# Attention's 0/1 selection matrices stored by ScalarE in the first graph sum and loaded by SyncE; gather indices taken further ahead; the decoder laid over all 128 rows

## The reference, cut to what matters

```python
def gcn_conv(x, src, dst, ew, W, b):
    deg = segment_sum(ew, dst, num_segments=N)
    dis = where(deg > 0, rsqrt(maximum(deg, 1e-12)), 0.0)
    norm = dis[src] * ew * dis[dst]
    return segment_sum(norm[:, None] * (x @ W)[src], dst, num_segments=N) + b
h = relu(gcn_conv(layernorm(x), src, dst, ew, W1, b1))     # 64 features
z = relu(gcn_conv(h, src, dst, ew, W2, b2))                # 32 features
x = x + sigmoid(relu(z @ Wd1 + bd1) @ Wd2 + bd2)           # decoder: 32 -> 64 -> 256
...
ft = (layernorm(x) @ W).reshape(n, 8, 32)                  # attention
e = leaky_relu(a1[src] + a2[dst], 0.2)
ex = exp(e - segment_max(e, dst, n)[dst])
out = segment_sum(ft[src] * (ex / segment_sum(ex, dst, n)[dst])[:, :, None], dst, n)
x = x + elu(out)
```

## Time and profile before

| | us |
|---|---|
| median of 3 runs | 9041.6 |
| lowest and highest run | 9036.97, 9072.32 |
| profiled execution, its own time | 9062.31 |
| its span, first to last instruction | 9060.6 |
| first graph sum, gathers | 562 to 2644 |
| second graph sum, gathers | 2796 to 4884 |
| decoder | 4889 to 5060 |
| mixture and projection | 5060 to 5893 |
| attention | 5893 to 8326 |
| the rest (elu, choice, feed-forward) | 8326 to 9061 |

### The profile page before, as it was taken

The page is one execution under the profiler, slowest core; times in us unless marked ns, Lnnn a source line. Parts: engine busy times, 40 slices in busy tenths (PEclk is TensorE's granted clock), DMA queues, the critical chain, the costliest instruction groups (busy, mean ns, idle before and its releaser), DMA issues. The chain is left out here.

```text
span 9060.6 us, 136786 instructions
## 1 busy us (share of the span) xinstructions
PE 5409.2 (60%) x23137; PEld 4141.3 (46%) x23138; DVE 4883.5 (54%) x14105; ACT 1604.5 (18%) x3526; POOL 5076.7 (56%) x5289
## 2 busy tenths in 40 slices
PE   4744444444453444444436899868888888885079
PEld 3643333333343333333334455645656556554046
DVE  6854444444443333333334433278888888888831
ACT  1200000000000000000002333423333333333511
POOL 0037777777754777777774000067677677774241
PEclk5555555555555555555555799977787787787589
DMA  3111111111102000000000000244444444443420
GB/s 71 33 28 26 26 26 26 26 26 26 26 18 72 13 13 13 13 13 13 13 13 8 16 21 19 71 125 130 128 132 132 127 130 128 131 130 107 142 76 20
DMA packets 380970, 523.06 MB, mean 58 GB/s; under 512 B 148710, under 2 KB 278046, under 8 KB 380700
## 3 DMA queue, kind: packets, MB, share of 16 engines
q0 software_dynamic: 198928, 349.25, 15.0%
q1 hardware_dynamic: 180812, 170.51, 6.0%
q10 hardware_dynamic: 960, 0.00, 0.0%
HBM read 450.68 MB, written 68.72 MB: 57 GB/s over the span
## 5 line engine op out<-in xcount | busy, mean ns | idle before, releaser
L694 POOL DMA_INDIRECT conv_rows<-table,conv_idx x3328 | 3157.1, 949 | 1181.5 <-issue 1010.9
L747 PE MATMUL conv_pm<-conv_rows,conv_sel 128*128 x7040 | 1704.5, 415 | 2539.9 <-SPq L710 2539.9
L747 PEld LDWEIGHTS conv_pm<-conv_rows,conv_sel 128*128 128x128 f32 x7040 | 1566.9, 328 | 2677.5 <-issue 2677.5
L1572 POOL DMA_INDIRECT att_rows<-ft_rows,att_idx x1760 | 1693.8, 962 | 1704.4 <-ACT att_idx L1586 1168.3
L736 DVE TENSOR_TENSOR acc<-acc,conv_pm 128x64 f32 (+1 forms) x3520 | 718.2, 204 | 2012.6 <-PE conv_pm L747 1223.2
L1748 PE MATMUL att_pm<-att_rows,att_sel 128*128 128x264 f32 x3520 | 1272.7, 503 | 229.1 <-DVE sums L1884 178.3
L720 DVE TENSOR_SCALAR conv_sel<-iota,edges,edge_w 128x128 f32<-128x128 f32 x3528 | 1014.3, 357 | 493.1 <-issue 467.1
L1748 PEld LDWEIGHTS att_pm<-att_rows,att_sel 128*128 128x128 f32 x3520 | 772.7, 244 | 582.9 <-DVE sums L1884 359.2
L1884 DVE TENSOR_TENSOR sums<-sums,att_pm 128x264 f32 x1760 | 748.3, 425 | 165.8 <-PE att_pm L1748 111.5
L682 ACT ACTIVATE conv_idx<-sources 128x8 int32 x416 | 86.7, 208 | 4000.1 <-SPq L710 3018.7
L1853 DVE TENSOR_TENSOR att_rows<-att_rows,att_pwi 128x1056 f32<-128x1056 f32 x440 | 545.9, 1241 | 10.8 <-issue 10.3
(11 more groups left out here) (357 smaller groups left out, 5993.6 us busy)
## 6 DMA issues: line engine op xcount, KB each, us to landing
att_bc<-places SPq DMA_DIRECT2D x110, 512.0 KB
conv_rows<-table,conv_idx POOLq DMA_INDIRECT x3328, 2.3
att_rows<-ft_rows,att_idx POOLq DMA_INDIRECT x1760
ft_rows<-proj_ft SPq DMA_DIRECT2D x25, 544.0 KB, 3.0
x_normal<-elu_xr SPq DMA_DIRECT2D x25, 514.0 KB
x_spilled<-x_rows SPq DMA_DIRECT2D x25, 512.0 KB, 2.9
elu_xg<-x_spilled SPq DMA_DIRECT2D x25, 512.0 KB
t_xg<-x SPq DMA_DIRECT2D x24, 512.0 KB
```

What stands on the lines that cost most here:

```text
L694: pool.indirect_dma_start(out=rows[:, k, :], out_offset=None, in_=table, in_offset=bass.IndirectOffsetOnAxis(ap=idx[:, k:k + 1], axis=0)). ...
L747: ins = nc.tensor.matmul(pm[q][:, i, :], sel[:, q * QUAD + i, :], rows[:, ds(slots[i], 1), :].rearrange("p a c -> p (a c)"), start=True, s ...
L1572: pool.indirect_dma_start(out=rows[:, k, :], out_offset=None, in_=K.ftd, in_offset=bass.IndirectOffsetOnAxis(ap=idx[:, k:k + 1], axis=0)). ...
```

## The change

**First graph sum.** With `keep=True` (conv1 alone) ScalarE also makes the unweighted selection matrices of all 1760 steps: |destination - column| by eight Abs operations for a section, then Relu(1 - that) over all eight, and stores the section's two quads to DRAM, through two buffers `hot`. In both sums the index ring has four sections instead of sixteen, and a copy waits for gathers up to 24 before its section.

**Attention.** `hots` and its semaphore are gone. SyncE loads each quad's matrices from DRAM; the load of quad q for block b + 1 is issued when TensorE has done quad q of block b. The index ring has 18 sections, filled at the start and refilled one whole ring ahead; GpSimd itself waits for TensorE (`mm_done`) before it gathers into used slots.

**Decoder.** The four windows' 32 latent features lie side by side on the 128 rows: one transpose for the group instead of four, and four matmuls of 128 columns with a zero-padded Wd1 of 128 rows instead of one of 512 columns with 32 rows. `dt` and Wd2 are padded with zeros to 128 rows. The bias is loaded four times and Wd1 four times.

```diff
-def graph_sum(nc, K, name, table, acc, C, x=None):
+def graph_sum(nc, K, name, table, acc, C, x=None, keep=False):
+    AHEAD = 4 * SECT
...
-        idx = ph.sb("idx", [P, SLOTS], I32)
+        idx = ph.sb("idx", [P, AHEAD], I32)
+        hot = ph.sb("hot", [P, 2, SECT, P]) if keep else None
+        stored = [ph.sem(f"stored{h}") for h in range(2)]
...
         @block.scalar
         def _(act):
+            def ones_of(b, j):
+
+                first, half, section = b * AHEAD + j * SECT, j % 2, b * (AHEAD // SECT) + j
+                act.wait_ge(stored[half], (b * (AHEAD // SECT // 2) + j // 2) * 16 + 16)
+                for k in range(SECT):
+                    ins = act.activation(hot[:, half, k, :], K.iota[:, :], ACT.Abs,
+                                         bias=K.edges[:, 1, ds(first + k, 1)], scale=-1.0)
+                ins.then_inc(apart, 1)
+                act.wait_ge(apart, section + 1)
+                act.activation(hot[:, half, :, :], hot[:, half, :, :], ACT.Relu, bias=K.ones[:, 0:1], scale=-1.0
+                               ).then_inc(made, 1)
+                act.wait_ge(made, section + 1)
+                act.dma_start(K.seld[ds(section * 2, 2)].rearrange("q p f -> p q f"),
+                              hot[:, half, :, :].rearrange("p (q i) n -> p q (i n)", i=QUAD)).then_inc(stored[half], 16)
...
+            with act.Fori(0, TB * P // AHEAD) as b:
+                for j in range(AHEAD // SECT):
+                    t = b * AHEAD + j * SECT
                     act.wait_ge(mm_done, t + (UNROLL - LAG + 1))
-                    act.wait_ge(arrived, t + SECT)
+                    act.wait_ge(arrived, t + (SECT + LANES - AHEAD))
                     act.activation(idx[:, j * SECT:(j + 1) * SECT], K.srct[:, ds(t, SECT)], ACT.Copy
                                    ).then_inc(idx_ready, 1)
+                    if keep:
+                        ones_of(b, j)
+            if keep:
+                for b in range(TB * P // AHEAD, STEPS // AHEAD):
+                    for j in range(AHEAD // SECT):
+                        ones_of(b, j)
+                for h in range(2):
+                    act.wait_ge(stored[h], 16 + STEPS // SECT // 2 * 16)
...
-        w1t, b1t = ph.sb("w1t", [CH2, CH1]), ph.sb("b1t", [CH1, 1])
-        w2t, b2t = ph.sb("w2t", [CH1 + 1, D]), ph.sb("b2t", [CH2, 1])
+        w1t, b1t = ph.sb("w1t", [P, GW, CH1]), ph.sb("b1t", [CH1, 1])
+        w2t, b2t = ph.sb("w2t", [P, D]), ph.sb("b2t", [P, 1])
-        zt = [ph.sb(f"zt{i}", [CH2, GW * P]) for i in range(2)]
-        dt = [ph.sb(f"dt{i}", [CH1 + 1, GW * P]) for i in range(2)]
+        zt = [ph.sb(f"zt{i}", [P, P]) for i in range(2)]
+        dt = [ph.sb(f"dt{i}", [P, GW * P]) for i in range(2)]
...
+            for i in range(GW):
+                sp.dma_start(b2t[i * CH2:(i + 1) * CH2, :], b2.unsqueeze(1)).then_inc(loaded, 16)
+            sp.wait_ge(zeroed, 1)
+            for i in range(GW):
+                sp.dma_start(w1t[i * CH2:(i + 1) * CH2, i, :], wd1).then_inc(loaded, 16)
...
             def turn(g, h):
                 pe.wait_ge(scaled, g + 1)
+                nc.tensor.transpose(pt[:, :], u[h][:, :, :].rearrange("p w c -> p (w c)"), K.ident[:, :]).then_inc(turned, 1)
+
+            def widen(g, h):
                 for i in range(GW):
-                    ins = nc.tensor.transpose(pt[:, i * P:(i + 1) * P], u[h][:, i, :], K.ident[:, :])
-                ins.then_inc(turned, 1)
-
-            def widen(g, h):
-                nc.tensor.matmul(pd[:, :], w1t[:, :], zt[h][:, :], start=True, stop=True).then_inc(d_done, 1)
+                    ins = nc.tensor.matmul(pd[:, i * P:(i + 1) * P], w1t[:, i, :], zt[h][:, :], start=True, stop=True)
+                ins.then_inc(d_done, 1)
...
+            def selections(n, q):
+
+                sp.dma_start(sel[:, q * QUAD:(q + 1) * QUAD, :].rearrange("p i n -> p (i n)"),
+                             K.seld[ds(n * NQ + q, 1)].rearrange("a p f -> p (a f)")).then_inc(sel_loaded[q], 16)
...
+            def body(b, more, most, further):
                 if most:
                     sp.wait_ge(m_ready, b + 2)
                     flags(b + 2)
-                    if not isinstance(b, int) or b + 3 < NB:
+                for q in range(NQ):
+                    if q == 2 and further:
                         sp.wait_ge(t_ready, b + 3)
                         places(b + 3)
-            blocks(sp, body)
+                    if more:
+                        sp.wait_ge(mm_done, b * SEGS + (q + 1) * QUAD)
+                        selections(b + 1, q)
...
-            def section(turn, j):
-
-                pool.wait_ge(idx_ready, turn * SECTS + j + 1)
+            def section(n, j, free=None):
+
+                pool.wait_ge(idx_ready, n + 1)
+                if free is not None:
+                    pool.wait_ge(mm_done, free)
...
                     act.wait_ge(mm_done, b * SEGS + (k + 1) * SECT)
-                    if not isinstance(turn, int) or 2 * b + k + SECTS < STEPS // SECT:
-                        take(b * 2 + (k + SECTS), (2 * i + k) % SECTS)
+                    if not isinstance(turn, int) or 2 * b + k + AHEAD < STEPS // SECT:
+                        take(b * 2 + (k + AHEAD), 2 * i + k)
...
-                    pe.wait_ge(sel_ready, b * NQ + q + 1)
+                    pe.wait_ge(sel_loaded[q], b * 16 + 16)
...
-            def hots(n, q):
-
-                s, at = n * SEGS + q * QUAD, q * QUAD
-                tt(sel[:, at:at + QUAD, :], count.unsqueeze(1).to_broadcast([P, QUAD, P]),
-                   K.edges[:, 1, ds(s, QUAD)].unsqueeze(2).to_broadcast([P, QUAD, P]), ALU.is_equal
-                   ).then_inc(sel_ready, 1)
...
+        K.seld = dram("selections", [STEPS // QUAD, P, QUAD * P])
```

More of the change, by code:

```diff
@@ L669, in graph_sum @@
         gathered = [ph.sem(f"gathered{k}") for k in range(LANES)]
-        idx_ready, taken, sel_ready, mm_done, added, arrived, zeroed, x_loaded = (
-            ph.sem(x_) for x_ in ("idx_ready", "taken", "sel_ready", "mm_done", "added", "arrived", "zeroed", "x_loaded"))
+        idx_ready, taken, sel_ready, mm_done, added, arrived, zeroed, x_loaded, apart, made = (
+            ph.sem(x_) for x_ in ("idx_ready", "taken", "sel_ready", "mm_done", "added", "arrived", "zeroed", "x_loaded",
+                                  "apart", "made"))
         block = ph.block()
@@ L875, in scale @@
                                   ).then_inc(scaled, 1)
+            own.did(dve.memset(w1t[:, :, :], 0.0))
+            own.then(dve.memset(w2t[CH1:P, :], 0.0))
+            dve.sem_inc(zeroed, 1)
             for h in range(2):
+                own.then(dve.memset(dt[h][CH1:P, :], 0.0))
                 dve.memset(dt[h][CH1:CH1 + 1, :], 1.0).then_inc(ones_set, 1)
@@ L902, in _ @@
             act.wait_ge(ones_set, 2)
-            act.wait_ge(loaded, 16 * 5)
+            act.wait_ge(loaded, 16 * LOADS)
             def latent(g, h):
@@ L944, in _ @@
             turn(1, 1)
-            pe.wait_ge(loaded, 16 * 5)
+            pe.wait_ge(loaded, 16 * LOADS)
             widen(0, 0)
@@ L1475, in attention @@
     PERIOD, LONG = 3, 9
+    AHEAD = 2 * LONG
     H1 = HD + 1
@@ L1544, in flags @@
                                  ).then_inc(th_loaded, 16)
+            def selections(n, q):
+                sp.dma_start(sel[:, q * QUAD:(q + 1) * QUAD, :].rearrange("p i n -> p (i n)"),
+                             K.seld[ds(n * NQ + q, 1)].rearrange("a p f -> p (a f)")).then_inc(sel_loaded[q], 16)
             places(0)
+            for q in range(NQ):
+                selections(0, q)
             sp.wait_ge(set_up, 1)
@@ L1553, in _ @@
             places(2)
-            def body(turn, i, more, most):
-                b = block_of(turn, i)
+            def body(b, more, most, further):
                 if most:
@@ L1646, in weights @@
                 act.activation(pw, df[:, 0:P], ACT.Exp).then_inc(p_ready, 1)
-            act.activation(count, K.iota[:, :], ACT.Copy).then_inc(counted, 1)
-            for j in range(SECTS):
+            for j in range(AHEAD):
                 take(j, j)
@@ L1922, in body @@
                 where = places(b, 2)
-                if more:
-                    hots(n, 0)
                 add(b, 2, where)
```

68 lines of the change are left out of this document (35 added, 33 removed).

## The result

| | before | after |
|---|---|---|
| median of 4 runs, us | 9047.1 (9037.0 to 9072.3) | 8947.3 (8938.5 to 8952.3) |
| profiled execution / span, us | 9062.3 / 9060.6 | 8945.5 / 8943.8 |
| first gather to last, first sum | 2081.5 | 2080.7 |
| last gather of the first sum to ScalarE's first operation of the next stage | 13.2 | 26.1 |
| gathers, second sum | 2087.3 | 2080.4 |

The ratio of the medians is 0.9882, 95% interval 0.9867 to 0.9898: faster by 1.2%. The spans differ by 116.8 us: 12.9 lost behind the first sum, and 0.8, 6.9, 39.4 and 87.1 gained in both sums' gathers, the decoder and the attention. All the other stages together take 4.5 us more. The central forecast asked for 176 us; 117 came by the two spans and 100 by the medians, since the profiled execution of before was 15 us above its own median.

What follows compares the result with a forecast made beforehand. It took GpSimd's gather issue to bound the graph sums, late feeding and release the attention, and low-clock TensorE the decoder. Terms 15 - 141 - 50 = -176 us gave 8866 us; own range 8817 to 8900, with rivals 8810 to 8960.

Steps and rivals of the forecast that it cites:

- The first sum: First graph sum: ScalarE's new sections of 4.1 us stay hidden until the end, then a tail costs +15 us.
- about twelve of them behind the last gathers: First graph sum, sign of being right: ScalarE's sections take 4 to 5 us, about twelve behind the last gathers.
- The bound of 5.5 us: First graph sum, upper bound: a ScalarE section takes 5.5 us, each dynamic address costing some 0.17, giving +33 us.
- the third rival: First graph sum: ScalarE becomes the bound, from 10.0 us a section; at 12 us, +240, 9282 us; chance 0.05.
- The second sum: Second graph sum: only the index ring gets shorter, so the time changes by 0.
- The decoder: Decoder: using all rows lifts TensorE's granted clock from 0.50 to 1.00, VectorE is the next bound; -50 us.
- the group: Decoder: a group of four windows falls from 6.46 to 4.2 us, 25 groups giving 56 us before 6 are deducted.
- The attention: Attention: without compares and with earlier release, blocks fall from 21.6 us to near GpSimd's issue floor of 20.0; -141 us.
- With some jitter I take 20.35: Attention: block time taken as 20.35 us, from 20.25 plus jitter; 107 x 1.25 = 134 us saved.
- the two-block loop: Attention: gathers, landing, a1, scans, TensorE's sums and next block's first eight steps take 40.5 us, 20.25 a block.
- The handoff: Attention: GpSimd is released by TensorE itself instead of through ScalarE's index copy, 1.0 us earlier.
- the second rival: Attention: bursts of loads delay gather landings, loop 1.2 us longer, 20.95 us a block; -112, 8930 us; chance 0.21.

Runs made afterwards that it cites:

- experiment 5: Two kernels: changed kernel with the decoder's wide product at 65 rows (decoder 157.1 us); kernel before with only that product padded to 128 rows (147.6 us).
- the 65-row run: Changed kernel with the decoder's wide-product operands (dt, w2t) at 65 rows again, all else kept but their zeroing; decoder 157.1 us.
- experiment 6: Changed kernel, but in the first sum ScalarE makes two sections of selections beside each of the first twelve index copies; 11985.7 us beside 11944.2 before.
- the run without reloads: Changed kernel loading only the first block's attention selections, used for all blocks; the run without the standstill took 8951.8 us beside 9049.2 before.
- experiment 1: Changed kernel loading only the first block's attention selections, used for all blocks; first run 12124.8 us beside 12107.6 before, second 8951.8 beside 9049.2.
- the handoff alone, second run: Kernel before with attention indices 18 sections ahead and GpSimd waiting for TensorE itself, compares kept on VectorE; second run 11905.1 us beside 11960.6 before.
- experiment 7: Kernel of experiment 6, with attention's GpSimd waiting for the matmuls of overwritten slots by four gathers instead of eight; 11377.9 us beside 11960.6 before, ratio 0.9516.

## Why the prediction was right or wrong

**The first sum was right.** Section 4.08 us against 4.1, stage end 13 us later against 15. An Abs of 128x128 took 386 ns (363 by the line through the two rows), the Relu 1148 (1120), the issue 0.38 (0.34). Thirteen sections ran behind the last index copy (2607.0), as in the sum; only the last four of them ended behind the last gather's start, so the sign "about twelve of them behind the last gathers" was wrongly worded. The bound of 5.5 us had no ground: no run shows 0.17 us for a dynamic address, and eight Abs take 2.44 us with dynamic addresses (inside the loop) and without (in the tail). Nor had the third rival (ScalarE as the bound): ScalarE waited some 6.2 us ahead of each section.

**The second sum** gained 6.9 us where I had 0. GpSimd waits for nothing there in either kernel; its gathers took 950.4 ns in the mean before and 946.2 after, which is the 6.9 us. In experiment 5's second kernel, whose second sum is the old one, they took 945.2, though under the standstill. So nothing shows that the change did it.

**The decoder was right in cause, 11 us off in size.** The clock rose, and experiment 5 shows that the rows did it. By the Trainium skill, "TensorE: Matmul & The Clock Gate", section "Why this matters for your kernels", being continuously busy would be enough; the 65-row run, busy 136 of 139 us at 0.52, disagrees, as the decoder of before did. The mis-sized term is the group: 4.47 us in the mean and not 4.2. Even at a granted 1.00 it is 4.45 to 4.58, for no engine is full (VectorE is busy 63.6 of 85 us and TensorE 62.8), so a group is a chain of waits and not VectorE's work alone; and the clock dips, in 4 of the 24 groups here and in 11 of experiment 6's decoder, where a group takes 4.89 in the mean. The old group's 6.46, one pitch of two rows, was 6.30 in the mean with its two short last ones. So 24 x (6.30 - 4.47) = 44 us came where I had 56; from the stage's start to its first Sigmoid it takes 1.7 us more than before and behind its last 2.9, against the 6 that I took off.

**The attention was wrong by 54 us.** The step that failed is "With some jitter I take 20.35". What it named as next was right: it was the two-block loop. Its parts, in the sum and as the trace has them:

| us | forecast | before | after |
|---|---|---|---|
| sixteen gathers, first start to last | 20.0 | 19.26 | 19.13 |
| last gather's start to the end of TensorE's eighth sum of the next body | 20.5 | 22.40 | 20.91 |
| from there to the waiting gather's start | 0 | 1.47 | 0.81 |
| loop, a block: half of these three | 20.25 | 21.56 | 20.43 |
| GpSimd's own pace, a block | 20.0 | 20.51 | 20.39 |
| block, reckoned as below | 20.35 | 21.65 | 20.86 |
| block measured | | 21.63 | 20.87 |

So three terms were off. GpSimd's own pace in the attention is not the graph sums' 20.0: its gathers take 958 ns in the mean and not 944, and 14 times in 107 blocks it stands, mostly for 1.51 us, ahead of a block's second gather, for nothing that the trace shows. Rows of the changed kernel (page, waits as above, timeline):

```profile
L1629 POOL DMA_INDIRECT att_rows<-ft_rows,att_idx x1760 | 1686.8, 958 | 1590.1 <-ACT att_idx L1646 972.7
...
POOL att_rows L1629 <- issue: 519.7, 1636, 1.5
...
6017.41 0.94 POOL L1629 DMA_INDIRECT att_rows<-ft_rows,att_idx  x1 [0.66 <-PE att_pm L1806]
...
6019.87 0.94 POOL L1629 DMA_INDIRECT att_rows<-ft_rows,att_idx  x1 [1.51 <-issue]
```

The loop was 0.18 us a block longer than I had. The handoff, which I priced at 1.0 us, gives 0.66 (1.47 less 0.81; the sum didn't use that price), and the way to the eighth sum fell by 1.5 where I had 1.28. In the mean the loop got 1.13 us a block shorter, 0.75 of it by that way and 0.33 by the handoff; that is an estimate from the two traces, for no run without the standstill has one half alone. The largest term is the spread: a block starts either one block at GpSimd's own pace after the block before, or one loop after the start of the block before that, whichever is later. Worked through with the 104 ways of the trace this gives 20.86 us a block; with each of them at their mean it gives 20.43. The difference, 0.43 us, is the price of the spread, and I had put 0.10. The same reckoning gives 20.87 for the run without reloads, measured 20.87, and 21.65 for before. It is worked out from the traces and not from a run that varied the spread. The ways go from 17.9 to 25.9 us, and at GpSimd's own pace one of up to 20.8 costs nothing; GpSimd can't make up in a short block what it lost in a long one, because in a short one it is at its pace already. The median block is 20.48; 20.35 was nearly a median, and I used it as a mean.

What makes a block long can be followed in one of 25.5 us. Timeline of the changed kernel:

```profile
7528.95 0.26 ACT L1655 ACTIVATE att_a<-att_rows 128x64 f32<-128x64 f32 x1 [3.81 <-DMA att_rows<-ft_rows,att_idx]
...
7529.26 0.47 PE L1758 MATMUL att_pxr<-ident,att_a 128*128 128x128 f32 x1 [4.39 <-ACT att_a L1655]
...
7532.71 2.13 PE L1806 MATMUL att_pm<-att_rows,att_sel 128*128 128x264 f32 x4
...
7534.63 6.83 PE L1774 MATMUL att_pma<-a,att_sel_t 128*128 x32
...
7550.84 0.94 POOL L1629 DMA_INDIRECT att_rows<-ft_rows,att_idx  x1 [5.51 <-PE att_pm L1806]
...
7553.41 1.15 PE L1806 MATMUL att_pm<-att_rows,att_sel 128*128 128x264 f32 x4
```

and its windows:

```profile
7525.40:7530.00 4.60, 0.74 (x2) 0.47 (x3) 1.95 (x5) 0.26 (x1) 3.69 (x4) 0.84 0.85 254
7530.00:7535.00 5.00, 5.00 (x15) 3.10 (x14) 3.19 (x6) 0.61 (x3) 3.78 (x5) 0.50 0.49 145
7535.00:7540.00 5.00, 5.00 (x25) 5.00 (x25) 3.22 (x5) 0.91 (x4) 3.59 (x5) 0.50 0.63 157
7540.00:7545.00 5.00, 5.00 (x18) 4.05 (x19) 0.97 (x2) 0.45 (x2) 3.78 (x5) 0.50 0.42 113
7545.00:7551.00 6.00, 5.55 (x15) 3.81 (x16) 4.58 (x15) 2.95 (x5) 0.49 (x2) 0.67 0.32 86
```

TensorE had caught up with the gathers. It stood 4.39 us for a copy that waited for a landing, and was granted 0.50 after that, for some 15 us in which it was busy throughout. Two sums (four records) then took 2.13 us where they take 1.15, and GpSimd, on time until then, stood 5.51. Over 106 blocks the granted clock and the length go together: the 52 blocks at 0.80 or more average 20.4 us, the twelve below 0.70 average 22.5. TensorE's idle time before the turned heads grew from 0.76 us a block to 1.87 (1.66 without reloads); 17 blocks have over 3 us of it, against 3 before. The Trainium skill describes such an oscillation, a wait for a transfer and then work at the low clock, in "TensorE: Matmul & The Clock Gate", section "HAM oscillation — how this bites in real kernels"; this block's rows agree. That the idle causes the low clock, and that causes the long blocks, is read from order and correlation; no run varied it.

So the second rival's number was the better one (20.95 us a block, 8930; measured 20.87, 8947) by luck, for its reason was wrong: experiment 1 takes the loads away and the block stays. Landings did grow, by 0.4 us, and cost nothing that can be seen.

## What to carry to other kernels

When a change takes an engine down to a floor, read the floor from that engine's own pace in that very stage (20.39 us a block here and not 20.0), and don't price the next loop by its mean: with GpSimd at its pace every long pass is lost and no short one is won back, so work the passes through one by one. A kernel that gets closer to its loads also lets TensorE idle in new places, and its clock may be part of the price. On TensorE, check the granted clock before counting columns: here padding one product's operands with zeros to 128 rows took 22 us off a stage of 170 in which TensorE had been busy without a gap.

## What the runs showed of the hardware

In eleven of the twelve experiments the kernel before ran 32 to 34% longer, and every version beside it was held up too. Timeline of the handoff alone, second run:

```profile
9009.91 1.01 PE L1733 MATMUL att_pcf<-ones,att_rc 1*128 1x1 f32 x4
...
9012.14 2.12 PE L1755 MATMUL att_pm<-att_rows,att_sel 128*128 128x264 f32 x4 [1.22 <-issue]
...
9020.29 0.95 POOL L1576 DMA_INDIRECT att_rows<-ft_rows,att_idx  x1 [0.30 <-issue]
9023.82 0.28 ACT L1640 ACTIVATE att_a<-att_pma 128x128 f32<-128x128 f32 x1 [16.23 <-DMA conv_rows<-table,conv_idx]
...
9024.30 0.48 DVE L1834 TENSOR_TENSOR_SCAN att_my<-att_fl,att_cc,att_mx 128x128 f32<-128x128 bf16 x1 [11.91 <-ACT att_cc L1647]
...
9024.40 0.56 PE L1746 MATMUL att_pcf<-att_pe_row,att_sel 1*128 1x8 f32 x2 [10.14 <-ACT att_cc L1647]
...
9033.38 0.94 POOL L1576 DMA_INDIRECT att_rows<-ft_rows,att_idx  x1 [12.14 <-PE att_pm L1755]
```

GpSimd goes on gathering at 1.25 us while ScalarE stands 16 us with its operand ready (the sums that att_a reads were done by 9010; the releaser that the row names belongs to a much earlier stage). VectorE and TensorE then wait for ScalarE's next copy, att_cc. ScalarE goes on 3.5 us after the sixteenth gather has started, when GpSimd itself has run out of free slots. ScalarE stands so once a block, 102 times in this run, for 15 us in the mean. In the graph sums VectorE and TensorE have waits of 1 to 6 us for nothing that the trace names. Releasing GpSimd by four (experiment 7) makes it pause twice a block, 3.8 and 3.1 us, instead of once for 12, and the block falls by 5.5 us. The feed-forward, which gathers too, takes 466 us instead of 370. The mixture, the projection and the decoder, which don't gather, keep their times to 1.5 us (the mixture 681 us in both conditions). What holds the engines back, the trace doesn't say. Nor is it shown to be a matter of the chip: the run without the standstill (experiment 1, second) and the kernel before at 11,960 us are recorded under the same chip number, 19 minutes apart.
